# Graph attention over sorted edges: one exponential per edge, turned weights in two sets of banks, products one supertile behind

## The reference

```python
h_src, h_dst = nfeats[src], nfeats[dst]
z_att = concat([h_src, h_dst, efeats])
e = leaky_relu(z_att @ W_attn + b_attn, 0.01)[:, 0]
m = concat([h_src, efeats]) @ W_ne
emax = segment_max(e, dst)
ex = exp(e - emax[dst])
alpha = ex / segment_sum(ex, dst)[dst]
z = segment_sum(alpha[:, None] * m, dst)
out = relu(concat([nfeats, z]) @ W_out)
x = layernorm(x + out)
```

## Time and profile before

| | us |
|---|---|
| median of three runs (lowest, highest) | 4924.11 (4914.36, 4927.84) |
| profiled execution, device time | 4937.21 |
| profiled execution, span of the trace | 4935.4 |
| POOL busy | 3304.1 (67%) |
| DVE busy | 2651.7 (54%) |
| ACT busy | 2267.7 (46%) |
| PE busy | 2110.4 (43%) |

### The profile page before, as it was taken

One profiled execution on the slowest core, in us unless ns is written; L12 is line 12 of the kernel. 1 busy time (PEld: TensorE's weight loads), 2 busy tenths in 40 slices (PEclk: granted clock), 3 DMA queues, 4 the chain that ended last, 5 costly groups with the idle time before them and its releaser, 6 DMA issues.

```text
span 4935.4 us, 65300 instructions
## 1 busy us (share of the span) xinstructions
PE 2110.4 (43%) x10260; PEld 1948.9 (39%) x10261; DVE 2651.7 (54%) x5260; ACT 2267.7 (46%) x4123; POOL 3304.1 (67%) x3149
## 2 busy tenths in 40 slices
PE   1444444444443444444444444444443444344446
PEld 0444434434433433334334333443333434343436
DVE  5555555555555555555555555555554555555557
ACT  1544445544444444445444444444444444444444
POOL 6566666666767766667666766666666677666751
PEclk8666666666566666566655656666666666666666
DMA  4444444444444444444444444444444444444441
GB/s 112 122 129 128 128 124 136 129 129 133 134 127 124 139 129 127 129 129 139 123 123 139 129 133 125 132 136 126 131 129 118 139 132 137 127 131 129 129 129 54
DMA packets 409572, 628.94 MB, mean 127 GB/s; under 512 B 208412, under 2 KB 208796, under 8 KB 409332
## 3 DMA queue, kind: packets, MB, share of 16 engines
q1 hardware_dynamic: 296164, 519.51, 32.8%
q0 software_dynamic: 100096, 102.60, 11.4%
q10 hardware_dynamic: 13072, 4.80, 0.5%
HBM read 621.58 MB, written 4.81 MB: 127 GB/s over the span
## 4 chain that ended last, share of the span: by engine, by line
issue 29%; DVE 20%; another core or an unknown queue 18%; DVEq 15%; ACT 12%; ACTq 5%; PE 1%; POOL 0%
DVE u L636 5%; DVE e L705 4%; DVE prod L631 4%; DVEq L760 3%; ACT psS L506 2%; ACT pT L468 2%; DVEq L727 2%; DVEq L698 2%; ACTq L520 2%; ACT acc L478 2%; DVE acc L698 2%; ACT zs L515 2%; ACT zb L516 1%; DVE bounds L750 1%
## 5 line engine op out<-in xcount | busy, mean ns | idle before, releaser
L373 POOL DMA_INDIRECT V<-in_x_dram,srcs x3128 | 3278.7, 1048 | 1509.2 <-issue 904.3
L866 PE MATMUL psT<-ident,e 128*128 128x128 f32 x3136 | 829.7, 416 | 2764.5 <-DVE e L705 1528.6
L866 PEld LDWEIGHTS psT<-ident,e 128*128 128x128 f32 x3136 | 597.5, 216 | 2921.0 <-DVE e L705 1601.7
L872 PE MATMUL psG<-V,pT 128*128 x6288 | 1367.0, 389 | 0.0
L872 PEld LDWEIGHTS psG<-V,pT 128*128 128x128 f32 x6288 | 1312.4, 306 | 0.1
L468 ACT COPY pT<-psT 128x512 f32<-128x512 f32 x785 | 451.5, 575 | 1410.0 <-remote 1364.1
L631 DVE TENSOR_TENSOR prod<-V,wa 128x512 f32<-128x512 f32 x782 | 506.8, 690 | 587.2 <-issue 587.1
L705 DVE TENSOR_TENSOR e<-zb,zs 128x1024 f32<-128x1024 f32 x392 | 478.8, 1221 | 268.5 <-remote 191.8
L746 DVE CUSTOM_DVE_ANT_0 um<-ubc,psS 128x1024 f32<-128x1024 f32 x391 | 477.4, 1221 | 157.8 <-issue 88.6
L636 DVE TENSOR_REDUCE u<-prod 128x8 f32<-128x1024 f32 x391 | 477.0, 1220 | 46.2 <-issue 12.1
L698 DVE SCALAR_TENSOR_TENSOR acc<-psG,half,acc x788 | 244.7, 349 | 396.9 <-issue 259.2
(11 more groups left out here) (97 smaller groups left out, 615.9 us busy)
## 6 DMA issues: line engine op xcount, KB each, us to landing
ubc<-scores SPq DMA_DIRECT2D x391, 512.0 KB
dbc<-in_dst_dram SPq DMA_DIRECT2D x390, 512.0 KB
V<-in_edge_attr_dram SPq DMA_DIRECT2D x390, 256.0 KB
V<-in_x_dram,srcs POOLq DMA_INDIRECT x3128
scores<-u SPq DMA_DIRECT2D x391, 4.0 KB
srcs<-in_src_dram SPq DMA_DIRECT2D x390, 4.0 KB
out_dram<-y SPq DMA_DIRECT2D x12, 256.0 KB
xt<-in_x_dram ACTq DMA_DIRECT2D x6, 448.0 KB
```

The source lines that it names most:

```text
L373: nc.gpsimd.indirect_dma_start(Vx[0:n, s, j, 0:F], None, x[:, :], bass.IndirectOffsetOnAxis(ap=srcs[0:n, s, j:j + 1], axis=0)).then_inc(h_ ...
L866: last = nc.tensor.transpose(psT[:, i, j * P:(j + 1) * P], e1[:, :].rearrange("q (p j) -> q j p", j=J)[:, 4 * i + j, :], ident[:, :])
L872: last = nc.tensor.matmul(psG[:, bass.ds(bk, 1), 0:AW].rearrange("p a f -> p (a f)"), pT[:, i, j * P:(j + 1) * P], V[:, bass.ds(sv + XW * ...
```

## The change

- The leaky score is formed before the exponential: ACT computes `psS = SLOPE * um + wnode[4]` (Identity), DVE computes `um = max(um + wnode[3], psS)`, and ACT does one exponential of it, into `e1`. `zb`, `zs`, the `max` after them and `ebias` are gone; `node` and `wnode` have five columns, with the scores unnegated in two of them.
- The turned weights have two sets of two banks in PSUM (`psT` of 4 banks); `psG` is one bank instead of two, `psR` is gone. PE's window is now: turn both halves, then multiply both halves, with the weights of the supertile before. ACT copies the set of the supertile before, both halves after the exponential.
- DVE merges first in its part of a supertile, and frees the slot itself: it waits for `agg_done` and raises `v_free` (`BEHIND = 3` now, the slot of the supertile three before).
- The attention weights `wa` that DVE multiplies by (`wa_v`) lie in PSUM, in the bank `psM` that the node pairs also use; so PE waits for DVE's product before a node pair, and DVE waits for the pair before the next product.

The core of the diff ("..." marks what is left out):

```diff
-BEHIND = 2
+BEHIND = 3
...
-        psT = ps("psT", [P, 2, 512])
-        psG = ps("psG", [P, 2, 512])
-        psR = ps("psR", [P, 512])
+        psT = ps("psT", [P, 4, 512])
+        psG = ps("psG", [P, 512])
...
-        wa_v = wa[:, :].rearrange("p (k f) -> p k f", f=F)[:, 0:3:2, :]
+        wa_v = psM[:, 0:2 * F].rearrange("p (k f) -> p k f", f=F)
...
# ACT, one supertile
                     nc.scalar.activation(psS[:, :], dbc[:, s % 2, :], ACT.Square, bias=nbias[:, 0:1], scale=FAR).then_inc(sq_done, 1)
+                    act.wait_ge(wn1, G)
+                    act.wait_ge(cmax_done, G)
+                    nc.scalar.activation(psS[:, :], um[:, :], ACT.Identity, bias=wnode[:, 4:5], scale=SLOPE).then_inc(low_done, 1)
+                    act.wait_ge(nn_done, G)
+                    nc.scalar.activation(dif[:, :], wnode[:, 2:3], ACT.Identity, bias=nn[:, 0:1], scale=-1.0).then_inc(dif_done, 1)
...
+                    rescale(G)
+                    act.wait_ge(tr[0], G)
+                    act.wait_ge(tr[1], G)
+                    act.wait_ge(lr_done, G + 1)
+                    nc.scalar.activation(e1[:, :], um[:, :], ACT.Exp, bias=nn[:, 0:1]).then_inc(e_done, 1)
+                    weights_out(G, 0)
                     weights_out(G, 1)
-                    rescale(G)
...
-                    nc.scalar.activation(zs[:, :], um[:, :], ACT.Exp, bias=ebias[:, 1:2], scale=SLOPE)
-                    nc.scalar.activation(zb[:, :], um[:, :], ACT.Exp, bias=ebias[:, 0:1]).then_inc(e_done, 1)
-                    weights_out(G, 0)
# DVE, one supertile
+                if left >= 1:
+                    dve.wait_ge(agg_done, dve.snap(g))
+                    dve.sem_inc(v_free[(s - BEHIND) % RING], 1)
...
+                    merge(G)
                     dve.wait_ge(node_set, G)
                     dve.wait_ge(u_in[r], scored)
-                    dve.wait_ge(e_done, G)
+                    dve.wait_ge(dif_done, G)
+                    dve.wait_ge(lr_done, G)
...
-                    weigh(G)
...
-                    merge(G)
+                    dve.wait_ge(low_done, G)
+                    nc.vector.scalar_tensor_tensor(um[:, :], um[:, :], wnode[:, 3:4], psS[:, :], ALU.add, ALU.max).then_inc(lr_done, 1)
...
+                    if y_steps is not None:
+                        dve.wait_ge(y_ready, y_steps + 1)
                     edge_product(s2).then_inc(prod_done, 1)
# PE, one supertile
+                if turns:
+                    free = pe.snap(room)
+                    pe.wait_ge(pt[0], free)
+                    pe.wait_ge(pt[1], free)
+                    pe.wait_ge(e_done, G + 1)
+                    turn(0, r)
+                    turn(1, r)
+                pe.wait_ge(merged, G + 1)
+                for i in range(2):
+                    pe.wait_ge(pt[i], G + 1)
+                    multiply(i, sv)
...
                 if ahead:
-                    nc.tensor.transpose(psR[0:32, 0:P], ident[:, 0:32], ident[:, :]).then_inc(v_free[(s - BEHIND) % RING], 1)
...
                     if s < YS:
+                        pe.wait_ge(prod_done, RING * k + s + 1)
                         y_pair(YS * k + s)
```

More of the change, by code:

```diff
@@ L133, in graph_attention @@
         nbias = sb("nbias", [P, 1])
-        wnode = sb("wnode", [P, 3])
+        wnode = sb("wnode", [P, 5])
         slopes = sb("slopes", [P, 3])
@@ L464, in weights_out @@
             def weights_out(G, i):
+                turned = act.snap(banks[1], min_val=0, max_val=2)
                 act.wait_ge(tr[i], G)
-                act.wait_ge((agg_half, agg_done)[i], G)
-                nc.scalar.copy(pT[:, i, :], psT[:, i, :]).then_inc(pt[i], 1)
+                act.wait_ge((agg_half, agg_done)[i], G + 1)
+                nc.scalar.copy(pT[:, i, :], psT[:, bass.ds(turned + i, 1), :].rearrange("p a e -> p (a e)")).then_inc(pt[i], 1)
             def rescale(G):
-                bb = act.snap(block_of[LAG], min_val=0, max_val=NB - 1)
-                sl = act.snap(slots[LAG], min_val=0, max_val=LAG)
+                bb = act.snap(block_of[LAG - 1], min_val=0, max_val=NB - 1)
+                sl = act.snap(slots[LAG - 1], min_val=0, max_val=LAG)
                 act.wait_ge(lowf_in, 16)
@@ L487, in pass_on @@
                 act.reg_mov(slots[0], act.snap(spare))
+                act.reg_mov(banks[1], act.snap(banks[0]))
                 act.reg_add(g, g, 1)
@@ L585, in _ @@
             nc.vector.memset(node[:, NB:NB + 1, 0:2], 0.0)
+            nc.vector.memset(node[:, NB:NB + 1, 3:5], 0.0)
             nc.vector.memset(alpha[:, :, :], 1.0)
@@ L624, in _ @@
                 step(dot(b, n, 1, node[:, b:b + n, 0]))
-            step(nc.vector.tensor_scalar(node[:, 0:NB, 0], node[:, 0:NB, 0], ba[:, 0:1], -1.0, ALU.add, ALU.mult))
+            step(nc.vector.tensor_scalar(node[:, 0:NB, 3], node[:, 0:NB, 0], ba[:, 0:1], None, ALU.add))
+            step(nc.vector.tensor_scalar(node[:, 0:NB, 0], node[:, 0:NB, 3], -1.0, None, ALU.mult))
             step(nc.vector.tensor_scalar(node[:, 0:NB, 1], node[:, 0:NB, 0], SLOPE, None, ALU.mult))
+            step(nc.vector.tensor_scalar(node[:, 0:NB, 4], node[:, 0:NB, 3], SLOPE, None, ALU.mult))
             def edge_product(s):
@@ L659, in _ @@
             dve.wait_ge(wz_copied, 1)
[L660 to L665, removed]
+            nc.vector.memset(psG[:, :], 0.0).then_inc(agg_done, 1)
+            for i in range(2):
+                nc.vector.memset(psT[:, i:4:2, :], 0.0).then_inc(tr[i], 1)
+            dve.wait_ge(agg_done, 1)
+            dve.sem_inc(agg_done, 1)
+            dve.sem_inc(agg_half, 2)
             dve.sem_inc(e_done, 1)
-            dve.sem_inc(merged, 1)
+            dve.sem_inc(dif_done, 1)
+            dve.sem_inc(lr_done, 1)
+            dve.sem_inc(scaled, 1)
             dve.wait_ge(acc_cleared, 2)
@@ L697, in merge @@
                     row = accv[:, bass.ds(bb + i, 1), :].rearrange("p a f -> p (a f)")
-                    last = nc.vector.scalar_tensor_tensor(row, psG[:, bass.ds(bk, 1), 0:AW].rearrange("p a f -> p (a f)"), half[:, bass.ds(tb, 1), i], row, ALU.mult, ALU.add)
+                    last = nc.vector.scalar_tensor_tensor(row, psG[:, 0:AW], half[:, bass.ds(tb, 1), i], row, ALU.mult, ALU.add)
                 last.then_inc(merged, 1)
-            def weigh(G):
-                dve.wait_ge(e_done, G)
-                dve.wait_ge(tr[1], G)
-                nc.vector.tensor_tensor(e1[:, :], zb[:, :], zs[:, :], ALU.max).then_inc(mx_done, 1)
             def pass_on():
@@ L749, in supertile @@
                     dve.wait_ge(wn1, G)
-                    nc.vector.scalar_tensor_tensor(bounds[:, :], slopes[:, :], cmax[:, 0:1], wnode[:, :], ALU.mult, ALU.add).then_inc(bounds_done, 1)
+                    nc.vector.scalar_tensor_tensor(bounds[:, :], slopes[:, :], cmax[:, 0:1], wnode[:, 0:3], ALU.mult, ALU.add).then_inc(bounds_done, 1)
                     dve.wait_ge(bounds_done, G)
```

131 lines of the change are left out of this document (54 added, 77 removed).

## The result

The changed kernel takes 5684.1 us (median of 4 runs, 5653.5 to 5710.3) beside 4922.1 us for the kernel before on the same chip: ratio 1.155, 95% interval 1.149 to 1.161. The forecast was 4833 us, in a range of 4400 to 5080. The time is outside it, on the side of rival B.

What follows compares the result with a forecast made beforehand. POOL's chain of gathers and waits was taken to bound the kernel. 4937.2 - 282 + 186 + 5 = 4846 us, or 4833 us against the median, 13.1 us below the profiled execution; range 4400 to 5080.

Steps and rivals of the forecast that it cites:

- rival B: POOL's slots, now released behind DVE and ACT: each burst of gathers starts late, kernel slower, 5020 us; chance 0.28.
- Gathers get shorter, -282: POOL's gathers: without DVE instructions reading two SBUF tiles beside them, 0.825 us less for each of 342 supertiles, 282 us.
- Length of pauses, 0: POOL's 569 us of pauses in the loop: taken as unchanged, the term the forecast knew least.
- next to nothing late: Bound on the pauses' term: PE's signals hardly late, all of POOL's pauses in the loop go, -569 us.
- 3.7 us until DVE may start `um`: ACT's copies, loop end, `nbias` and square after held signals arrive, against 1.9 us in the smooth order.
- Node pairs, +186: 49 supertiles with a node pair: added waits make them 16.0 us instead of 12.20, +186 us.
- DVE's and ACT's own work, 0: DVE's stream 9.4 us a supertile, covered by POOL's 10.0, so no cost.
- Start, +5: Start of the kernel: supertile 0's slot comes free some 4 us later and four more banks are cleared, +5 us.
- over 3 us in mean: Sign towards the slower rival: POOL's pauses as many or more, over 3 us in the mean, `um` waiting for ACT's square.
- The point at which it decides: POOL's pauses longer by 0.27 us per supertile, from which on late-starting bursts decide.
- the hold: PE's signals arriving late, 13 us in one place, while POOL issues gathers back to back, and coming free once POOL pauses.

Runs made afterwards that it cites:

- e7: The changed kernel, but PE frees the slots again, after its products; 4289.3 us, ratio 0.988, on the chip where the kernel before takes 4342.8 us.
- e8: The kernel before, but DVE frees the slots at its own start and PE's small transpose goes; 4257.0 us beside 4342.8 us, ratio 0.980.
- e3: The changed kernel without the 3040 gathers of the loop; 4045.2 us, one run.
- e13: The changed kernel with the slots freed by PE, as e7, on a chip where the kernel before takes 4921.7 us; 5160.0 us, ratio 1.048.
- e15: The changed kernel itself, run again; 5701.7 us beside 4921.7 us for the kernel before, ratio 1.158.
- e17: The kernel before with the slots freed by DVE, as e8, on a chip where the kernel before takes 4853.5 us; 4963.8 us, ratio 1.023.
- e9: The changed kernel itself, run again; 5750.7 us beside 4938.3 us for the kernel before, ratio 1.167.

## Why the prediction was wrong, step by step

- *Gathers get shorter, -282*: right. Mean 944 ns; 325.9 us less. The small `wnode` instruction, which stayed, left nothing visible of the 90 us at most that were set beside this term. Where POOL runs without pauses the gain shows (10.0 against 10.6 us a supertile, e7 and e8); in the changed kernel the pauses took it three times over.
- *Length of pauses, 0*: this is the step that failed, as the term that I knew least. POOL's waits went from 605 to 1665 us. The bounds took "next to nothing late" on one side and rival B on the other, and B's price was too low: "3.7 us until DVE may start `um`" counted ACT's queue at its quiet 1.1 us, where in a long row of gathers it takes 9 us (3003.68 to 3013.01). Idle times of over 1 us before a gather of the loop are 235 of 7.0 us in the mean, where the kernel before has 208 of 2.7. The supertiles without pairs took 13.8 us where 11.2 to 11.5 were forecast.
- *Node pairs, +186*: size right (15.4 us in e3, 16.0 forecast; with steps (15.8 - 0.3 x 13.8)/0.7 = 16.6).
- *DVE's and ACT's own work, 0*: right with POOL's 10.0 us as cover; own pace 9.09 us in e3 (9.4 forecast), and 8.8 us between the two supertiles after the last gather, where the kernel before has 9.17 and 9.2 to 9.7 was forecast.
- *Start, +5*: right; the first gather that needs a freed slot starts at 149.5 us, 143.1 before.
- Rival B named the right place, a burst that starts late because ACT stands with its queue ahead of the square and DVE frees slots only at its own start, and its sign of "over 3 us in mean" came true. Its size, 5020, missed by 660 us. The point at which it decides, 0.27 us more of pause a supertile, was passed ten times over.
- What I read wrongly in the rows: "I don't know from the trace why PE's signals are held" treated the hold as PE's. The trace of before already had 755 steps on DVE and 498 on SP. My reading of how the change brought it out: taking ACT off PE's signals took it off the wait that had hidden the crawl. Before, ACT stood 1364 us in waits for PE, and went through its queue mostly after POOL had paused (116 us ahead of `nbias`); now it goes through the queue in the middle of the row. The waits of the two traces fit this; no run tried ACT's new order alone.

Not settled: what makes the queues crawl. Instruction fetches were as many with steps as without (392 packets in e7 and in e13), so it is not their number. Every time here comes from an execution that has a trace, so it isn't shown either that the crawl comes without the recording of the trace. Also open: whether length or rate of the gathers does it; why one chip is free of it (the kernel before wasn't traced there); what the whole change does on such a chip; and how much of the last 4 to 5% of e13 is ACT's new order.

## What to carry to other kernels

Before moving register work, branches and loads of an engine, look at its queue rows, not only its compute rows: where a wait goes, that work moves to another moment, and here the moment decided between 0.035 and 0.70 us apiece. Don't take an "issue" piece before an instruction for a fixed cost without a look at its longest beside its mean (0.9 and 0.3 us on POOL before; 13.7 and 5.1 us on ACT after). Release a shared slot from the engine that is done with it first (e13 against e15, 542 us), and measure such a change on more than one chip: e8 gained 2.0% on one and the same kernel, e17, lost 2.3% on another.

## What the runs showed of the hardware

- During rows of back-to-back indirect gathers of POOL, register moves, register arithmetic, branches, loads and waits of ACT, DVE, SP and PE went in part in steps of 0.70 us, where a register move takes 0.035 us otherwise. In the changed kernel 891 of 1001 did so between 12 and 16 us after a row's start, in the kernel before 200 of 1780; with the gathers left out there were 3. The gathers of the changed kernel kept their 0.944 us and 0.30 us between them.
- The kernel before took 4916, 4938, 4922 and 4854 us on four chips, where at least one kernel's trace has steps by the hundred, and 4343 us on a fifth, where four kernels' traces have at most 44. The same kernel took 4289 us there (e7) and 5160 us on one of the four (e13).
- A pause of POOL ends it, but for a few: once it had lasted 2.5 us, none of 7230 register, branch and load instructions stepped in the changed kernel's trace, and 13 of 7421 when it was run again (e9).
